# Attention with 64-row score tiles, a head pitch of 37 and outputs made transposed

## The reference, cut to what matters

```python
x = tokens(images)                                  # (64, 37, 256)
# layer l, attention, 16 heads of 16 channels
q, k, v = split(norm(x) @ Wqkv)
a = softmax(causal(q @ k.T / sqrt(16) + bias))      # per image and head, 37 x 37
x = x + (a @ v) @ Wout + bout
# layer 0: shared expert + top 2 of 7 experts; layer 1: silu(x g) * (x u) d
x = x + ffn(norm(x))
```

## Time and profile before

| | us |
|---|---|
| median of 2 runs | 1297.4 (1295.07 to 1299.74) |
| profiled execution | 1297.63, of which the span from first to last instruction 1295.4 |
| PE busy (matmul) | 1150.3, 89% of the span |
| PEld busy | 967.9, 75% |
| DVE busy | 699.3, 54% |
| ACT busy | 636.0, 49% |
| POOL busy | 444.9, 34% |
| chain of waits | PE 67%, DVE 9%, POOL 8%, issue 6%, ACT 4%, DMA 4% |

### The profile page before, as it was taken

How to read it: one execution, slowest core, us unless ns; L and a number is a source line. 1 busy time by engine, 2 the same in 40 slices (tenths; PEclk the granted TensorE clock), 3 DMA queues, 4 the chain that set the end, 5 groups by cost and what they waited for, 6 DMA issues and landing times.

```text
span 1295.4 us, 24968 instructions
## 1 busy us (share of the span) xinstructions
PE 1150.3 (89%) x8484; PEld 967.9 (75%) x8485; DVE 699.3 (54%) x1366; ACT 636.0 (49%) x1083; POOL 444.9 (34%) x334
## 2 busy tenths in 40 slices
PE   6989999989998887899999999961789998979998
PEld 5877777766676665788888888851567777769998
DVE  3257777663332324566666666620467767764443
ACT  3455555534333433455555555530465554535554
POOL 3255443513344533011122111113554555341110
PEclk9999999988998988899999999985899999989999
DMA  6550000007111112010111111103000000000000
GB/s 217 178 208 2 1 0 0 1 11 285 20 25 22 29 21 82 28 33 33 36 33 33 37 33 33 33 29 108 30 22 20 19 19 0 1 1 10 19 19 29
DMA packets 30786, 56.93 MB, mean 44 GB/s; under 512 B 12892, under 2 KB 22314, under 8 KB 29588
## 3 DMA queue, kind: packets, MB, share of 16 engines
q1 hardware_dynamic: 16184, 44.06, 9.8%
q0 software_dynamic: 13328, 10.66, 3.1%
q10 hardware_dynamic: 1228, 1.59, 0.4%
HBM read 41.50 MB, written 14.67 MB: 43 GB/s over the span
## 4 chain that ended last, share of the span: by engine, by line
PE 67%; DVE 9%; POOL 8%; issue 6%; ACT 4%; DMA 4%; SPq 0%; DVEq 0%; POOLq 0%; ACTq 0%
PE ps L1174 26%; PE ps L1179 11%; PE ps L1181 10%; PE ps L1180 10%; POOL routed_in L444 6%; PE ps L1288 4%; DVE Sb L834 2%; DMA yg<-routed_out 2%; PE ps L1540 2%; DVE mx L832 2%; DVE Sb L829 2%; PE ps L1281 2%; POOL xn L378 1%; PE ps L1304 1%; ACT vts L593 1%
## 5 line engine op out<-in xcount | busy, mean ns | idle before, releaser
L372 POOL TENSOR_TENSOR Km<-KT,cst 128x592 f32<-128x592 f32 x128 | 156.0, 1250 | 101.5 <-ACT KT L593 93.7
L468 POOL DMA_INDIRECT routed_out<-yt,tile_to x43 | 65.4, 1521 | 289.9 <-DVE yt L1109 285.7
L1087 DVE TENSOR_TENSOR tile_w<-arena,tile_w 128x1408 fp32r<-128x1408 f32 x86 | 139.3, 1621 | 35.6 <-ACT tile_w L770 35.6
L1174 PE MATMUL ps<-arena,shared 128*128 x516 | 130.9, 395 | 1.0 <-ACT shared L766 1.0
L1179 PE MATMUL ps<-tile_w,xTs 128*128 128x352 f32 x344 | 120.0, 349 | 2.5 <-DVE xTs L1092 2.5
L770 ACT ACTIVATE tile_w<-arena 128x1408 fp32r x86 | 118.2, 1376 | 6.5 <-issue 6.5
L926 DVE TENSOR_TENSOR Hd<-Sg,ps 128x296 f32<-128x296 f32 x96 | 44.4, 462 | 137.2 <-ACT Sg L711 134.0
L378 POOL TENSOR_TENSOR xn<-cen,rsd 128x592 f32<-128x592 f32 x32 | 46.7, 1460 | 192.8 <-ACT rsd L565 192.7
L1181 PE MATMUL ps<-tile_w,xTs 128*128 128x352 f32 x344 | 112.0, 326 | 0.0
L1174 PEld LDWEIGHTS ps<-arena,shared 128*128 128x128 f32 x516 | 90.9, 189 | 28.3 <-issue 15.6
L1180 PE MATMUL ps<-tile_w,xTs 128*128 128x352 f32 x344 | 111.7, 325 | 0.0
(11 more groups left out here) (199 smaller groups left out, 2816.6 us busy)
## 6 DMA issues: line engine op xcount, KB each, us to landing
arena<-in_ew_dram SPq DMA_DIRECT2D x7, 2176.0 KB, 13.2
x_in<-in_xT_dram SPq DMA_DIRECT2D x7, 888.0 KB, 5.2
xt<-routed_in SPq DMA_DIRECT2D x43, 129.0 KB, 2.1
yg<-routed_out SPq DMA_DIRECT2D x8, 592.0 KB
out_dram<-h SPq DMA_DIRECT2D x8, 296.0 KB, 2.7
routed_in<-zero_x SPq DMA_DIRECT2D x13, 129.0 KB, 4.6
gu_i<-in_gu_dram SPq DMA_DIRECT2D x1, 1536.0 KB, 20.7
shared<-in_gu_dram SPq DMA_DIRECT2D x1, 1408.0 KB, 7.5
```

Source lines behind the costliest of these rows:

```text
L372: ins = pool.tensor_tensor(Km[p % 2][:, c], src, headmask.unsqueeze(2).to_broadcast([P, HG, W2]), ALU.mult)
L468: pool.indirect_dma_start(ys, bass.IndirectOffsetOnAxis(tile_to[b][:, 0:1], 0), yt[b][:], None).then_inc(s_yt, 16)
L1087: dve.tensor_tensor(tile_w[half][1], gate_up_of(w, half), tile_w[half][0].bitcast(F32), ALU.subtract).then_inc(s.wl, 1)
L1174: return pe.matmul(out_, lhsT, rhs, start=start, stop=stop)
```

## The change

The attention of both layers is built anew.

- Heads. The channels of Q and K are permuted on the host (by_half), so that each half of 64 rows of a chunk holds four whole heads of each of the two chunks. Km then has 4 heads per half in place of 8 per chunk: one instruction of POOL of 128x592 per pair in place of two. The scores are eight matmuls of 64 rows by 37 columns, moving 148 columns each, the row halves r into different banks.
- The pitch of heads is 37 in place of 64 in the exponentials and the values, so that no padding is cleared and transposes have 74 columns.
- The outputs are made transposed: the stationary side is the values (74 rows, 32 columns), the moving side the exponentials (74 x 37), and the result has channels in its rows. The two heads of a piece are kept apart by a mask (vmask) when ACT writes V, in two instructions of 128x296 in place of one of 128x592.
- Normalisation follows the transposed form: DVE takes the reciprocal of each sum 16 times over (128 x 16 spread to 128 x 256), TensorE transposes the reciprocals (two pieces), ACT copies them (shares_t), DVE multiplies outputs and shares (one instruction of 128 x 148). The transposes of the outputs (outputs_t) are gone.
- High and low half of the attention outputs are made once per group, on ACT (upper_out) and POOL (lower_out), in place of once per pair on ACT and DVE.
- The norm of a group is made two groups ahead (norm_ahead), with two buffers xa. The projections are spread over the group, K first. Two groups are merged and normed before the first scores.
- The order on every engine is new. On DVE it is, for each pair: normalise of the pair before, sums, scaling of the next pair's scores, then the reading of some bank (merging additions, centre, or residual), then maximum and subtraction.
- On POOL the low halves of the last feed-forward's weights stand behind the last lower_out.

The core of the diff:

```diff
+def km(a, g, p):
+    n = 4 * g + p
     pool.wait_ge(a.S_mm, n + 1)
...
+    if p == 0:
+        pool.wait_ge(a.proj, FREE + 6 * g + 2)
+    src = KT[:, :, p * W2:(p + 1) * W2].unsqueeze(2).to_broadcast([P, DK, HG, W2])
+    pool.tensor_tensor(Km[p % 2], src, headmask.unsqueeze(1).unsqueeze(3).to_broadcast([P, DK, HG, W2]),
+                       ALU.mult).then_inc(a.km, 1)
+def lower_out(a, g, gb):
+    pool.wait_ge(a.OTh, g + 1)
+    pool.tensor_tensor(OTs[1], OTn[gb], OTs[0].bitcast(F32), ALU.subtract).then_inc(a.OTs, 1)
...
+    def step(g, b, X, turn):
+        km(a, g, 3)
+        if not X.first:
+            lower_out(a, g - 1, 1 - b)
+        if X.last:
+            return
+        km(a, g + 1, 0)
+        if turn is not None:
+            sum_routed(g + 3, 1 - b, turn)
+        km(a, g + 1, 1)
+        norm(*norm_ahead(l, g, X), b)
+        km(a, g + 1, 2)
+        if not X.near:
+            lower_x(a, g + 2, b, xa[b])
+        elif l == 1:
             lower_x(F[1], 0, 0, xf1[0])
...
+    lower_out(a, GROUPS - 1, 1)
...
+    def project(g, k, bk):
         act.wait_ge(a.proj_mm, 6 * g + k + 1)
+        src = ps[:, bk, 0:N]
+        if k < DK:
+            act.wait_ge(a.km, FREE + 4 * g)
         if k < 2 * DK:
...
+            c = DK + k if k < DK else k - DK
+            act.activation((KT, QT)[k // DK][:, k % DK], src, ACT.Identity,
+                           bias=qkv_b[:, c:c + 1] if l == 0 else zero_t[:]).then_inc(a.proj, 1)
         else:
...
+            c = k - 2 * DK
+            for odd in range(2):
+                ins = act.activation(VT[:, c, :, odd], src.rearrange("p (i t) -> p i t", t=T), ACT.Identity, scale=vmask[:, odd:odd + 1],
+                                     bias=val_b[:, c, odd:odd + 1] if l == 0 else zero_t[:])
+            ins.then_inc(a.proj, 1)
...
+    def shares_t(n, p, bk):
+        act.wait_ge(a.O_mm, FREE + n + 1)
+        act.wait_ge(a.OTn, n + 1)
         src = ps[:, bk, 0:DK * P].rearrange("p (c i q) -> p c i q", c=DK, i=2)[:, :, :, 0:T]
...
+        act.activation(RTs[p % 2].rearrange("p c (i q) -> p c i q", i=2), src, ACT.Copy).then_inc(a.RTs, 1)
+    def upper_out(g, gb):
+        act.wait_ge(a.OTn, FREE + 4 * g + 4)
+        act.wait_ge(a.out_mm, FREE + 2 * g)
+        act.activation(OTs[0], OTn[gb], ACT.Copy).then_inc(a.OTh, 1)
...
+    def step(g, b, X):
         n = 4 * g
+        if not X.first:
+            shares_t(n - 1, 3, 6)
+        values(n, 0, 7)
+        probs_t(n, 0)
         values(n + 1, 1, X.bank("V1"))
...
         if not X.first:
...
+            upper_out(g - 1, 1 - b)
         if X.first and l == 1:
             dequantise_gate_up()
...
+        if not X.last:
+            project(g + 1, 0, X.bank("proj0"))
+            project(g + 1, 1, X.bank("proj1"))
+        exps(n + 1, 1)
+        shares_t(n, 0, X.bank("O0"))
         probs_t(n + 1, 1)
...
         if X.first and l == 1:
             upper_gate_up()
...
+        values(n + 2, 2, X.bank("V2"))
         if not X.last:
...
+            project(g + 1, 2, X.bank("proj2"))
+            project(g + 1, 3, X.bank("proj3"))
+            squares(*norm_ahead(l, g, X))
+        exps(n + 2, 2)
+        shares_t(n + 1, 1, X.bank("O1"))
         probs_t(n + 2, 2)
...
         if X.first and l == 1:
             dequantise_down()
+        values(n + 3, 3, X.bank("V3"))
         if not X.last:
...
+            deviation(*norm_ahead(l, g, X), X.bank("var"))
+            project(g + 1, 4, X.bank("proj4"))
         exps(n + 3, 3)
+        shares_t(n + 2, 2, X.bank("O2"))
+        probs_t(n + 3, 3)
         if X.first and l == 1:
             upper_down()
         if not X.last:
...
+            project(g + 1, 5, X.bank("proj5"))
+            if not X.near:
+                upper_x(a, g + 2, b, xa[b])
+            elif l == 1:
+                upper_x(F[1], 0, 0, xf1[0])
             exps(n + 4, 0)
...
+    def scaled(n, p):
         b = p % 2
         dve.wait_ge(a.S_mm, FREE + n + 1)
         dve.wait_ge(a.ex, n + 1)
...
+        halves_of = lambda t: t.rearrange("p (r h) k -> p r (h k)", r=2)
+        dve.scalar_tensor_tensor(out=halves_of(Sb[b]), in0=ps[:, 2 * b:2 * b + 2, 0:DK * HW], scalar=HD ** -0.5,
+                                 in1=halves_of(bias[l][:]), op0=ALU.mult, op1=ALU.add).then_inc(a.sb, 1)
...
+    def centred(n, p):
+        b = p % 2
         dve.wait_ge(a.sb, FREE + n + 1)
         dve.tensor_reduce(mx[b][:], Sb[b], AX_X, ALU.max).then_inc(a.mx, 1)
...
+        dve.tensor_tensor(Sb[b], Sb[b], mx[b][:].unsqueeze(2).to_broadcast([P, HEADS, T]),
                           ALU.subtract).then_inc(a.sc, 1)
...
     def sums(n, p):
         b = p % 2
         dve.wait_ge(a.ex, FREE + n + 1)
...
+        dve.tensor_reduce(sm[b][:], Pr[b], AX_X, ALU.add).then_inc(a.sum, 1)
+        dve.wait_ge(a.O_mm, n + 1)
         dve.wait_ge(a.sum, FREE + n + 1)
...
+        dve.reciprocal(rs[b], sm[b][:].unsqueeze(2).to_broadcast([P, HEADS, HD])).then_inc(a.rs, 1)
+    def normalise(g, n, p, gb, bk):
+        dve.wait_ge(a.RTs, FREE + n + 1)
+        if p == 0:
+            dve.wait_ge(a.OTs, g + 1)
+        dve.tensor_tensor(OTn[gb][:, :, p * W2:(p + 1) * W2],
+                          ps[:, bk, DK * P:DK * (P + W2)].rearrange("p (c q) -> p c q", c=DK), RTs[p % 2],
+                          ALU.mult).then_inc(a.OTn, 1)
...
+    def step(g, b, X):
         n = 4 * g
...
         if not X.first:
...
+            normalise(g - 1, n - 1, 3, 1 - b, 6)
         sums(n, 0)
...
+        scaled(n + 1, 1)
+        if X.comb:
+            add_routed(g + 2, 0, X.bank("comb0"))
+            add_routed(g + 2, 1, X.bank("comb1"))
+        centred(n + 1, 1)
+        normalise(g, n, 0, b, X.bank("O0"))
+        sums(n + 1, 1)
+        scaled(n + 2, 2)
+        if not X.last:
+            centre(*norm_ahead(l, g, X), X.bank("mean"))
+        else:
             residual(g - 1, 0, X.bank("out0p"))
             residual(g - 1, 1, X.bank("out1p"))
...
+        centred(n + 2, 2)
+        normalise(g, n + 1, 1, b, X.bank("O1"))
         sums(n + 2, 2)
...
+        scaled(n + 3, 3)
+        if not X.first and not X.last:
+            residual(g - 1, 0, X.bank("out0p"))
+        centred(n + 3, 3)
+        normalise(g, n + 2, 2, b, X.bank("O2"))
         sums(n + 3, 3)
...
         if not X.last:
...
+            scaled(n + 4, 0)
+        if not X.first and not X.last:
+            residual(g - 1, 1, X.bank("out1p"))
+        if not X.last:
+            centred(n + 4, 0)
...
+    normalise(GROUPS - 1, 4 * GROUPS - 1, 3, 1, last.bank("O3"))
...
+    def scores(n, g, p):
         pe.wait_ge(a.km, FREE + n + 1)
         pe.wait_ge(a.sb, n + 1)
+        if p == 0:
+            pe.wait_ge(a.proj, FREE + 6 * g + 4)
+        pe.sem_inc(s_scores, 1)
         for c in range(DK):
...
+            for r in range(2):
+                for i in range(2):
+                    rows, q0 = slice(r * R64, (r + 1) * R64), (2 * p + i) * T
+                    ins = mm(ps[i * PITCH:i * PITCH + T, 2 * (p % 2) + r, c * HW:(c + 1) * HW],
+                             QT[rows, c, q0:q0 + T], Km[p % 2][rows, c, :, i * T:(i + 1) * T])
         ins.then_inc(a.S_mm, 1)
...
     def outputs(n, p, bk):
+        pe.wait_ge(a.rs, FREE + n + 1)
+        for c in range(DK):
+            pe.transpose(ps[:, bk, c * P:(c + 1) * P],
+                         rs[p % 2][:, c * HP:(c + 1) * HP].rearrange("p h d -> p (h d)"), ident)
         pe.wait_ge(a.PTs, FREE + n + 1)
         pe.wait_ge(a.Vb, FREE + n + 1)
...
+        for c in range(DK):
+            for i in range(2):
+                for q in range(HG):
+                    at = DK * P + c * W2 + i * T
+                    ins = mm(ps[q * 2 * HD:(q + 1) * 2 * HD, bk, at:at + T],
+                             Vb[p % 2][:, i, c * P + q * 2 * HD:c * P + (q + 1) * 2 * HD],
+                             PTs[p % 2][:, c * HG + q, i * T:(i + 1) * T])
         ins.then_inc(a.O_mm, 1)
...
         probs_t(n, 0)
...
+        scores(n + 2, g, 2)
+        if X.comb:
+            at("comb0", lambda bk: routed_out(g + 2, b, 0, bk))
+        at("V1", values, n + 1, g, 1)
+        if X.comb:
+            at("comb1", lambda bk: routed_out(g + 2, b, 1, bk))
+        if not X.last:
+            at("proj0", project, g + 1, 1 - b, 0)
+            at("proj1", project, g + 1, 1 - b, 1)
         at("O0", outputs, n, 0)
...
         probs_t(n + 1, 1)
...
+        scores(n + 3, g, 3)
+        if not X.last:
+            if X.comb:
+                pe.wait_ge(C.h, 2 * g + 6)
+            at("mean", mean, *norm_ahead(l, g, X))
+            at("V2", values, n + 2, g, 2)
+            at("proj2", project, g + 1, 1 - b, 2)
+            at("proj3", project, g + 1, 1 - b, 3)
+        else:
+            at("V2", values, n + 2, g, 2)
             at("out0p", out_proj, g - 1, 0)
             at("out1p", out_proj, g - 1, 1)
...
         at("O1", outputs, n + 1, 1)
...
         probs_t(n + 2, 2)
...
         if not X.last:
...
```

(96 more changed lines are left out.)

325 lines of the change are left out of this document (110 added, 215 removed).

## The result

| | before | after |
|---|---|---|
| median of 2 runs, us | 1297.4 (1295.07 to 1299.74) | 1348.93 (1347.36 to 1350.51) |
| ratio, 95% interval | | 1.0397, 1.0344 to 1.045: slower |
| profiled execution, its span, us | 1297.63, 1295.4 | 1347.36, 1345.5 |
| PE, DVE, ACT, POOL busy, us | 1150.3, 699.3, 636.0, 444.9 | 1111.7, 724.5, 636.0, 382.7 |
| mean granted clock | 0.951 | 0.928 |

The account below looks back on a forecast made before the run. Attention was taken as bound by TensorE's order with a few us of waits, afterwards by DVE's ring; layer 0 +21.3, layer 1 +14.7, ends +1.7 and +9.4 sum to 47.1 us: 1345 us, range 1303 to 1385.

Parts of the forecast that it names:

- The reciprocal: DVE's divide for each pair, its input spread from 16 to 256 elements: 1.84 us where it was 0.253.
- The ring: Attention's loop where DVE's normalise waits for ACT's copy: steps 6.15, 8.10, 8.05, 6.50; a group 29.4 us against 26.7.
- Layer 1's end: POOL's low halves of feed-forward weights wait behind the last lower_out: first matmul 18.8 us after the last exponential, +9.4.
- The end of layer 0: From the last pair's exponential to the output projection, 6.4 us before: +1.7.
- The starts: Beginnings of both layers, second group's mean and variance against dropped masks and clearings: net 0, within 3 us.
- my third rival: TensorE loses its clock or tiles, or the reciprocal costs 2.3: group 31 to 32, 1375 to 1390 us; chance 0.10.
- unchanged or smaller: TensorE's total work in attention, at most 25.4 us a group, costed at nothing because TensorE waits in all four steps.
- a cheap divide: Rival: DVE's reciprocal streams at 0.50 us, TensorE and ACT set the pace; group 24.6, 1273 us; chance 0.13.
- covered banks: Rival: the two PSUM bank waits in attention's second and third steps are covered; group 26.5, 1307 us; chance 0.12.
- the merging additions: Two additions in DVE's first step in six groups of layer 1, with transposes and late outputs: 1.9 each, 11.4 us.

Follow-up runs that it names:

- Experiment 3: Changed kernel with POOL's low halves of the last feed-forward's weights put ahead of the last group's lower_out: 1342.82 us, ratio 1.0345 to the kernel before.
- Experiments 1 and 2: Changed kernel, separately with: reciprocal on 128x16 then a spreading copy, 1320.79 us; long reciprocal kept, mean, first output projection and their DVE readers moved early, 1328.0 us.
- experiment 4: Changed kernel with DVE's order of before, sum and reciprocal behind the next pair's scaling, maximum and subtraction: 1447.26 us, ratio 1.1146 to the kernel before.

## Why the prediction was right, step by step

- **The reciprocal**: forecast 1.84 us, measured 1.75. The row of 16 elements (0.253) and this one give (1.753 - 0.253) / 240 = 6.25 ns an element, against 6.6 from the 4-element row: it goes by elements written, spread ones too. The Trainium skill, "VectorE: DVE Perf Modes", section "First, the fixed hardware budget", gives a repeat count of 8; the estimate of 2.3 us worked out from it was too long by a third, and the measurement decides.
- **The ring**: forecast 6.15 for a step, and 8.10, 8.05 and 6.50 with what hangs on it. From 150.94 on the steps are 8.11, 6.34, 6.82, 8.04, 8.12, 6.32, 6.52 and 8.04; the group forecast at 29.4 took 29.3 and 29.0. What waits for what is as told, with one exception, the pieces of TensorE after the exponential (below). Two sums of the forecast are a little off: the terms of one step give 6.14, and those of the first group 26.55 and not 26.35 (measured 26.8).
- **Layer 1's end**: forecast 18.8 us from the end of the last exponential to the feed-forward, measured 1204.84 - 1187.06 = 17.8, with POOL's weights alone for 6.88 of it. The other 2.6 of the +11.0 are behind that point: the feed-forward starts at the 1.2 GHz level (0.45 for a matmul that then takes 0.30) and stays there for some 5 us, where before it left that level 0.8 us after its start; I had not priced this. Experiment 3 took away the wait and this with it.
- **The end of layer 0** came out at 308.19 - 300.59 = 7.6 us against 8.1. The starts did not net to 0: +2.1 in layer 0, and +2.3 ahead of layer 1 (the 3.5 less the 1.2 that the end of layer 0 grew by, 7.6 against 6.4), +4.4 together where I allowed 3.
- **The closeness of the sum is in part luck.** The starts' +4.4 and the unpriced clock at the end are in part made up by terms that came out smaller. In layer 1 the errors cancel as well: its first group took 30.6 us where the terms give 28.0, the next six 30.6 on average where they give 31.3, the last three steps 20.9 where they give 19.8.
- **The clock**, my third rival's condition, did fall, in places: the mean went from 0.951 to 0.928. In layer 1 the group at a granted clock of 0.85 took 32.45 us, two at 0.94 took 30.84 and 30.95, two at 1.00 with as many matmuls 29.95 and 30.20. The forecast had no term for it; it stayed far from the rival's 1375 to 1390.
- **TensorE**: "unchanged or smaller" was smaller. Busy time 79.5 to 50.2 us for the scores, 77.6 to 31.5 for the outputs, 75 us of TensorE in these two, 39 in all. I had said that the scores double if nothing overlaps; but a pass moves 148 columns where it moved 296, so twice the passes are the same number of columns. Little of the saving showed, because TensorE waited.
- **What would have failed**: my two rivals' prices. I took 24.6 a group and 1273 us for a cheap divide, and 26.5 and 1307 for covered banks. Experiments 1 and 2 put them at 27.4 and 1321, 27.9 and 1328. In both sums I let DVE's ring shrink alone; transposes, scores and the mean or projection stand in one row behind the exponential on TensorE, and POOL's instructions drift onto the subtraction. The same gap made both theories of experiment 4 wrong.

Left open: how much of layer 1's +14.0 is the merging additions alone. At a clock of 1.00 the groups with them take 29.95 and 30.20 us and the one without 28.91, so 1.0 to 1.3 each where I had 1.9, but no run separates them. Also what 64-row scores without transposed outputs would give, which was not tried.

## What to carry to other kernels

A cheaper engine is worth little while the ring around it grows: before one spreads a row of scalars by broadcasting it into a divide, divide the few and copy them, on the engine with room. A wait removed on one engine is only worth the next row of work on the others, so price the changes together: here 28 and 21 us alone were 67 together. In an in-order queue a long instruction can also fill a wait; moving it elsewhere (experiment 4) costs both.
